# Four x loads per batch: 32 partitions with four runs each, or 128 partitions with one run each

## What is computed

```python
c    = einsum('bsd,bdh->bsh', x, W[cat]) + bias[cat][:, None, :]
c    = act_qdq(c)                      # one scale: the largest |c| of all batches is needed first
up   = act_qdq(c @ lpbq_dequant(w_up).T)
gate = act_qdq(c @ lpbq_dequant(w_gate).T)
gate = act_qdq(gate * fixed_qdq_u16(sigmoid(gate)))
o    = act_qdq(gate * up)
out  = x + o @ lpbq_dequant(w_down).T
```

## Time and profile before

| | us |
|---|---|
| median of 3 runs | 992.97 (990.86 to 994.11) |
| the profiled execution | 986.85 |
| its span, first to last instruction | 985.0 |
| around the span | 1.85 |
| TensorE busy, of the span | 888.6 (90%) |
| VectorE busy | 656.9 (67%) |
| ScalarE busy | 434.3 (44%) |

### The profile page before, as it was taken

How to read it: one execution, slowest core, us unless ns; L and a number is a source line. 1 busy time by engine, 2 the same in 40 slices (tenths; PEclk the granted TensorE clock), 3 DMA queues, 4 the chain that set the end, 5 groups by cost and what they waited for, 6 DMA issues and landing times.

```text
span 985.0 us, 13129 instructions
## 1 busy us (share of the span) xinstructions
PE 888.6 (90%) x4644; PEld 471.3 (48%) x4644; DVE 656.9 (67%) x755; ACT 434.3 (44%) x534; POOL 3.1 (0%) x12
## 2 busy tenths in 40 slices
PE   8776887999999999999999999993039999999998
PEld 6766877444444444444444444441014444444445
DVE  3334778965457654439899799858999877756511
ACT  1212332632332323249889784226886544444000
POOL 0000000000000000000000000000000000000000
PEclk8999999999999999999999999997569999999999
DMA  8999996454356433469999854799988899978231
GB/s 246 318 297 295 284 282 183 162 170 151 130 179 234 138 118 117 144 251 359 424 397 411 310 209 160 300 424 410 419 333 311 324 330 339 339 274 323 86 107 43
DMA packets 95671, 254.37 MB, mean 258 GB/s; under 512 B 33746, under 2 KB 50386, under 8 KB 91794
## 3 DMA queue, kind: packets, MB, share of 16 engines
q1 hardware_dynamic: 60434, 198.73, 57.8%
q10 hardware_dynamic: 35200, 55.20, 16.0%
HBM read 173.94 MB, written 73.66 MB: 251 GB/s over the span
## 4 chain that ended last, share of the span: by engine, by line
PE 75%; SPq 11%; DMA 6%; issue 3%; ACT 3%; DVE 1%; ACTq 0%; POOL 0%; DVEq 0%
PE bank L859 16%; PE bank L860 16%; PE bank L861 16%; SPq L381 7%; PE bank L895 6%; PE bank L894 6%; PE bank L896 6%; DMA x_ring<-in_x_dram 3%; ACT umag L730 2%; DMA up_extra<-up_scratch 2%; SPq L387 1%; SPq L396 1%; PE wt_bank L896 1%; PE wt_bank L895 1%; PE wt_bank L894 1%
## 5 line engine op out<-in xcount | busy, mean ns | idle before, releaser
L636 ACT ACTIVATE stage<-bank 128x512 f32<-128x512 f32 x186 | 108.9, 594 | 213.9 <-PE bank L861 160.1
L789 PE MATMUL bank<-xt,w_ring 128*128 128x128 f32 x960 | 114.6, 278 | 30.8 <-DMA w_ring<-in_L_cond_W_dram 16.6
L1166 DVE TENSOR_REDUCE tile_max<-stage 128x1 f32<-128x1536 f32 (+1 forms) x62 | 108.4, 1749 | 35.2 <-ACT stage L636 32.1
L859 PE MATMUL bank<-xq_head,wt_gate 128*128 (+1 forms) x336 | 127.5, 380 | 0.1
L859 PE MATMUL bank<-xq_head,wt_up 128*128 x336 | 127.4, 379 | 0.2 <-ACT stage L636 0.2
L860 PE MATMUL bank<-xq_head,wt_gate 128*128 (+1 forms) x336 | 127.3, 379 | 0.0
L861 PE MATMUL bank<-xq_head,wt_gate 128*128 (+1 forms) x336 | 127.3, 379 | 0.0
L860 PE MATMUL bank<-xq_head,wt_up 128*128 x336 | 127.3, 379 | 0.0
L861 PE MATMUL bank<-xq_head,wt_up 128*128 x336 | 127.3, 379 | 0.0
L789 PEld LDWEIGHTS bank<-xt,w_ring 128*128 128x128 f32 x960 | 109.4, 192 | 35.8 <-issue 20.1
L991 DVE STREAM_TRANSPOSE xt<-x_ring 128x512 f32<-128x512 f32 x32 | 35.4, 1107 | 75.6 <-DMA x_ring<-in_x_dram 75.6
(11 more groups left out here) (228 smaller groups left out, 1342.3 us busy)
## 6 DMA issues: line engine op xcount, KB each, us to landing
up_ring<-up_scratch SPq DMA_DIRECT2D x54, 768.0 KB, 7.2
w_ring<-in_L_cond_W_dram SPq DMA_DIRECT2D x30, 1024.0 KB, 12.7
gate_scratch<-stage ACTq DMA_DIRECT2D x32, 768.0 KB, 3.3
gate_ring<-gate_scratch SPq DMA_DIRECT2D x32, 768.0 KB, 8.5
up_scratch<-stage ACTq DMA_DIRECT2D x30, 768.0 KB, 7.8
product_scratch<-prod_ring SPq DMA_DIRECT2D x19, 768.0 KB, 8.0
back_ring<-product_scratch SPq DMA_DIRECT2D x19, 768.0 KB, 13.1
gate_even<-gate_scratch SPq DMA_DIRECT2D x16, 768.0 KB, 7.9
```

Source lines behind the costliest of these rows:

```text
L636: nc.scalar.activation(stage[:, q % 2, n % PIECE_TILES, :], up_bank(i, n), ACT.Copy)\
L789: mm = nc.tensor.matmul(bank[:, m * S:(m + 1) * S], w_ring[:, r, k, m * P:(m + 1) * P], xt[:, r % XT, k, :], start=(k == 0), stop=(k == KH ...
L859: nc.tensor.matmul(bank, w_hi, x_hi, start=(k == 0), stop=False)
L1166: V.tensor_reduce(tile_max[:, side, bass.ds(Q * i + q, 1)], stage[:, q % 2, :, :].rearrange("p t c -> p (t c)"), AX.X, ALU.max, apply_abso ...
```

## The change

Each of the four loads of a batch takes one block t of 32 rows in place of one quarter q of the columns. The destination of a load is 128 partitions with one run of 512 bytes each, where it was 32 partitions with four runs of 512 bytes each. The source of a load is walked as 4 column quarters, each of 32 rows, where it was 32 rows p, each of 4 blocks t. The bytes, their places in `x_ring`, the number of loads, the semaphore and all waits stay.

```diff
--- before.py
+++ after.py
@@ -377,9 +377,9 @@
                     turned = held(sp, b - BPC + 1)
                     sp.wait_ge(idx_in, 16)
                     sp.wait_ge(x_turned, turned)
-                for q in range(QUADS):
-                    sp.dma_start(x_ring[32 * q:32 * q + 32, r, :, :],
-                                 x_flat[bass.ds(b, 1), :, q * P:(q + 1) * P].rearrange("a (t p) j -> p (a t) j", p=32))\
+                for t in range(QUADS):
+                    sp.dma_start(x_ring[:, r, t, :],
+                                 x_flat[bass.ds(b, 1), 32 * t:32 * t + 32, :].rearrange("a p (q j) -> q (a p) j", j=P))\
                         .then_inc(x_in[r], 16)
```

## The result

The changed kernel takes 1031.28 us at the median of 4 runs (1030.78 to 1034.06), beside 992.2 us before (four runs here, three in the table above): 39 us slower, ratio 1.0398 with an interval of 1.0371 to 1.0425. Its profiled execution takes 1031.75 us with a span of 1029.9 us, 44.9 us more than the 985.0 us of the span before.

The account below looks back on a forecast made before the run. It took DMA transfers in the conditional stage as the bound: on engines 0 to 3, 205 us times 1.12 gives 230 us against 158.5, +71, so 1064 us as median. Range 1026 to 1125 us, leaving 2 in 10 out.

Parts of the forecast that it names:

- Bound and placement: Conditional stage: transfers set the pace; each new x load uses the same 4 engines, not 16; four engines given 0.85.
- The price of x: x loads on engines 0 to 3: 18.3 GB/s per busy engine, 3.59 us per batch, 115 us in all.
- lower end: Stage loads on engines 0 to 3: unstretched 205 us, +47; with overlap of 1.07, 192 us, +33.
- Matrices alone: Matrix loads in the conditional stage: 25.4 GB/s per engine, 65.5 KB or 2.58 us per batch.
- The stretch: Slowdown of mixed x and matrix loads: 1.33 before, taken as 1.12 after, 205 us becoming 230, +71 us.
- the case of no stretch: Stage loads on engines 0 to 3 at their pace alone: 205 us, +47 us.
- 132 packets but a period under 6 us: Sign in SP's queue and transpose spacing: would show the price of an engine wrong; 6.5 to 8 us expected.
- The share: Sign in the conditional stage: mean DMA share drops from 1.07 to about 0.65, rate to some 200 GB/s.
- Rival 1: x loads stay on 16 engines, writes spread over 128 partitions: 9 to 20 us faster, 973 to 984 us; chance 0.08.
- Rival 2: x loads stay on 16 engines, stretch comes from short packets as such: no difference, 990 to 996 us; chance 0.07.
- Rival 3: Four engines, but stretch sits in x packets or engines 0 to 3 run empty: beyond 1125 us; chance 0.05.
- Clock: TensorE's clock may fall while idle between batches: costed at nothing, at most +3.3 us for the last batch.

Follow-up runs that it names:

- narrow4: Kernel before the change, old 32-partition destination, x source walked with an outermost count of 4, rows misplaced: 1054.19 us beside 987.4, ratio 1.0687.
- narrow8: Kernel before the change, old 32-partition destination, x source walked with an outermost count of 8, rows misplaced: 1003.68 us beside 987.4, ratio 1.0167.
- wide16: Changed kernel's 128-partition destination with a contiguous source on 16 engines, columns misplaced: 959.57 us beside 987.4 for the kernel before, ratio 0.9716.
- wide16q: Changed kernel's 128-partition destination with the old kernel's source walk on 16 engines, columns misplaced: 956.75 us beside 989.25 for the kernel before, ratio 0.9693.
- half: Kernel before the change with the new load form for every second batch (slots 0 and 2): 1008.75 us beside 988.51, ratio 1.023.
- halfact: half with all x loads issued early on ScalarE's queue, SP's keeping matrices and w_gate: 1018.46 us beside 987.34 for the kernel before, ratio 1.0314.
- order0213: Kernel before the change with each batch's x quarters loaded in the order 0, 2, 1, 3: 986.73 us beside 989.25, ratio 0.9995.

## Why the prediction was right, and where it was off

**Bound and placement: right.** The stage goes at the pace of the transfers; the wide loads get 4 engines; packets fall by 1536; the loss lies wholly ahead of the gate projection, and the stages behind it keep their length. narrow4 and narrow8 show the dealing along the outermost source count for two more values. The Trainium skill's rule for the number of engines ("DMA: Bandwidth & Descriptors", "Why a DMA increments its semaphore by 16 and not by 1") agrees with the counts 16, 8 and 4 measured here.

**The price of x: too high, because packets overlap.** For x alone I took 18.3 GB/s a busy engine, and busy it was: 86 GB/s at a share of 0.29 (the window 5 to 6 us above) is 18.5. But a share of 0.29 of 16 engines is 1.16 of the four that work: their packets overlap. So each of the four moves 21.5 GB/s, and a batch takes 3.0 us in place of 3.59. I had put such an overlap, 1.07, into the lower end only. Matrices alone: about 2.5 us as forecast.

**The stretch: smaller than taken.** I took 1.12 on 205 us, 230 us for the stage's loads, +71. The first gate matmul shows +44.7, that is 158.5 + 44.7 = 203 us. By my prices that is a stretch of 0.99, the case of no stretch, which the range held. With the measured price of x the unstretched sum is 187 us (97 for x), and the stretch is 203/187 = 1.08. So of the 27 us too many, some 20 come from the price of x and some 6 from the stretch. My reason for 1.12 went by the mean rate of the stage, and that is not how it works: in the changed kernel x and matrices hardly overlap, and each runs at about its pace alone.

**What the forecast's own signs say.** I had written: 132 packets but a period under 6 us, and the price of an engine is wrong. The packets came; the period is 5.84 to 6.04 us at the end and 6.31 on average, below the 6.5 to 8 that I gave, and the price was indeed off. The share (0.69 and 0.63) and the rate (237 and 218 GB/s) of the two windows lie near the forecast 0.65 and at or above the forecast 200.

**How much of the hit was luck.** The measured 1031 us lies 5 us above the lower end of a range 99 us wide. The placement was right by its mechanism; the size is in the range because that reached below the case of no stretch. The destination's own gain of 21 to 28 us is not a term of the sum. The kernel with the misplacement alone, narrow4, costs 67 us; that this is near the +71 bears nothing out, since the price of x in the sum was off.

**Rival 1 (better spreading) was false for this change but true as a mechanism.** I priced it at 9 to 20 us with the stretch gone. With 16 engines over 128 partitions it brings 28 to 32 us. TensorE was faster than I had set, 3.6 us a batch in place of 4.1; wide16's timeline has 181 matmuls without a gap:

```profile
99.82 20.38 PE L789 MATMUL bank<-xt,w_ring 128*128 128x128 f32 x181
```

Rival 2 (short packets as such) is refuted by wide16 and wide16q. Rival 3 did not occur: in the phases of x above the share stays at 2 tenths or more, so the four engines did not run empty.

**Clock.** I costed a fall at nothing except at most 3.3 us for the last batch. The last batch lost 1.6 us (5.44 against 3.81). Falls earlier in the stage (the long windows have 0.87 to 0.93) are not separated from the waits for loads; the loads set the pace there.

**Spread of the runs.** The profiled executions differ by 44.9 us and the medians by 39. Before the change the profiled execution was 5 to 6 us below the median, after it 0.5 us above. The median-to-median forecast of +71 should thus be held against +39, the trace's against +45.

## What to carry over

Ahead of making a DMA wider on the SBUF side, look at the outermost loop of both sides: in these runs the smaller count, where it was 4, 8 or 16, was the number of engines, and the packets of the queue divided by the number of loads show it (data runs plus one completion for each engine). If a busy share near 1 comes with a rate well below that of a single stream, compare with a permuted load that writes over all partitions: if the rate jumps, it is how the destination is laid out and not how short the packets are. A load that sits on few engines can leave the others idle each time it comes, as in half, and not only when those few have the most to do in all. When x alone is priced from a share, allow for packets that overlap: on four engines the share was 1.16 of them.

## What was unexpected about the hardware

- With 512-byte runs written into 32 partitions, four in each, the mixed stream moved 311 GB/s; with the same bytes and packets spread over 128 partitions, 388. x alone showed no such difference (18 GB/s for a busy engine in both).
- A DMA issue on ScalarE's queue held the engine for up to 7.2 us (halfact), where the median of the same line was 0.56 us. Behind the one of 5.34 us the engine's next bias copy came 8.22 us late.
- Alternating the quarters on one queue (order0213) changed nothing that could be measured, while separate queues for short and long packets gave 9 us.
- Reordering the rows of a load's source, with the same runs and 16 engines, lengthened its issue from 432 to 600 ns at the median and the kernel by 4 us.
